# Routing folded into its neighbour blocks: the first layer's beside the time steps, the second layer's in pieces among the projections

## What is computed

```
xn     = (x - mean(x)) / sqrt(var(x) + 1e-5)
logits = xn @ router + bias;  prob = softmax(logits)          # 8 experts
layer 0: e = argmax(prob);            gate = prob[e]
layer 1: e0, e1 = the two largest;    position of each token in its expert's list, dropped at 512
time steps: dt = softplus(logits_dt + dt_bias);  a = -dt * exp(A_log);  sums of a inside chunks of 128
layer 1:  q = xn @ Wq;  latent = (xn @ (Wk + Wv)) @ W_down;  k = latent @ W_up_k;  v = latent @ W_up_v
```

## Time and profile before

| what | value |
| --- | --- |
| median of 3 runs | 2052.54 us |
| profiled execution | 2049.56 us, span 2047.8 us |
| TensorE busy | 1803.0 us, 88% of the span |
| VectorE busy | 1381.2 us, 67% |
| ScalarE busy | 1159.0 us, 57% |
| GpSimd busy | 432.4 us, 21% |
| mean granted TensorE clock | 0.94 of full speed |

### The profile page before, as it was taken

The page is one execution under the profiler, slowest core; times in us unless marked ns, Lnnn a source line. Parts: engine busy times, 40 slices in busy tenths (PEclk is TensorE's granted clock), DMA queues, the critical chain, the costliest instruction groups (busy, mean ns, idle before and its releaser), DMA issues. The chain is left out here.

```text
span 2047.8 us, 33896 instructions
## 1 busy us (share of the span) xinstructions
PE 1803.0 (88%) x10070; PEld 1240.1 (61%) x10070; DVE 1381.2 (67%) x3090; ACT 1159.0 (57%) x2806; POOL 432.4 (21%) x406
## 2 busy tenths in 40 slices
PE   5389999999999889999844988999999898999998
PEld 2247657656766679999812454555556464656555
DVE  5648678768677612222165869798879888888885
ACT  2145665665565412222111538888888888888886
POOL 2004413422432334321110111020201002020101
PEclk9689899899899889999966999999999999999999
DMA  4412212312221188655173583252424333343311
GB/s 165 137 55 93 92 63 79 105 61 72 92 72 62 42 300 276 201 180 173 54 236 117 159 260 106 73 104 73 104 73 93 63 83 94 83 93 83 86 29 32
DMA packets 143790, 226.12 MB, mean 110 GB/s; under 512 B 17725, under 2 KB 110015, under 8 KB 143648
## 3 DMA queue, kind: packets, MB, share of 16 engines
q1 hardware_dynamic: 124464, 179.95, 29.1%
q0 software_dynamic: 19184, 44.45, 8.5%
HBM read 174.26 MB, written 50.99 MB: 110 GB/s over the span
## 5 line engine op out<-in xcount | busy, mean ns | idle before, releaser
L2286 DVE TENSOR_SCALAR att_scores<-att_psS 128x512 f32<-128x512 f32 x512 | 352.9, 690 | 95.3 <-PE att_psS L2116 94.8
L2235 ACT ACTIVATE att_prob<-att_scores,att_shift 128x512 f32<-128x512 f32 x512 | 383.2, 748 | 23.0 <-DVE att_shift L2302 22.9
L2244 ACT COPY att_pT<-att_psT 128x512 f32<-128x512 f32 x512 | 306.4, 599 | 132.5 <-PE att_psT L2124 131.9
L2294 DVE CUSTOM_DVE_ANT_0 att_scores<-att_scores,first_decay 128x512 f32<-128x512 f32 x512 | 352.0, 688 | 0.0
L2124 PEld LDWEIGHTS att_psT<-ident,att_prob 128*128 128x128 f32 x2048 | 244.8, 142 | 158.7 <-issue 97.6
L2124 PE MATMUL att_psT<-ident,att_prob 128*128 128x128 f32 x2048 | 315.1, 277 | 15.4 <-ACT att_pT L2244 14.8
L2116 PE MATMUL att_psS<-first_ks,first_qs 128*128 128x512 bf16 x512 | 195.8, 384 | 17.3 <-DVE att_scores L2286 13.5
L1123 ACT ACTIVATE mamba_L<-mamba_am,mamba_minus 128x128 f32<-128x128 f32 x512 | 153.9, 387 | 44.5 <-PE mamba_psY L998 44.4
L2138 PE MATMUL att_psO<-att_pT,att_v 128*32 128x512 f32 x1024 | 140.6, 624 | 37.8 <-ACT att_pT L2244 37.8
L1543 ACT ACTIVATE ffn_hT<-ffn_psH,ffn_b 128x128 f32<-128x128 f32 x156 | 44.7, 369 | 194.6 <-PE ffn_psH L1499 194.6
L1499 PEld LDWEIGHTS ffn_psH<-ffn_xT,ffn_w 128*128 128x128 f32 x1248 | 145.3, 192 | 3.6 <-DMA ffn_w<-in_w 0.9
(11 more groups left out here) (287 smaller groups left out, 2872.4 us busy)
## 6 DMA issues: line engine op xcount, KB each, us to landing
ffn_w<-in_w SPq DMA_DIRECT2D x39, 1024.0 KB, 5.6
mamba_am<-a_rows SPq DMA_DIRECT2D x64, 512.0 KB, 3.8
first_qs<-q_parts SPq DMA_DIRECT2D x256, 64.0 KB, 3.1
first_ks<-k_parts SPq DMA_DIRECT2D x256, 64.0 KB, 3.1
xn<-xn_all SPq DMA_DIRECT2D x16, 512.0 KB, 5.7
ffn_w<-in_w POOLq DMA_DIRECT2D x8, 1024.0 KB, 6.7
att_w<-in_inter POOLq DMA_DIRECT2D x7, 1024.0 KB, 5.5
att_w<-in_outer POOLq DMA_DIRECT2D x7, 1024.0 KB, 7.3
```

The lines of the kernel that those rows point to most:

```text
L2235: nc.scalar.activation(prob[:, n % NP], scores[:, n % NCL], ACT.Exp, bias=shift[:, h % 2, t:t + 1], accum_out=total[:, octet % 2, t, j, i: ...
L2244: nc.scalar.copy(pT[:, h % HEADS_T, :, t * P:(t + 1) * P], bank_of("turn", n)[:].rearrange("p (k q) -> p k q", k=CPB)).then_inc(pT_ready, 1)
L2286: vec.tensor_scalar(scores[:, n % NCL], psS[n % NS][:], -CLAMP, CLAMP, ALU.max, ALU.min).then_inc(clipped, 1)
L2294: vec.tensor_tensor_reduce(scores[:, n % NCL], scores[:, n % NCL], decay[:, FAR - t * P:FAR - t * P + SEQ], 1.0, -2.0 * CLAMP, ALU.mult, A ...
```

## The change

It takes `route` apart into a class `Router`, whose methods are pieces of the same arithmetic, with a few `step`s turned into `link`s. In layer 0 the pieces stand inside the block of the time steps. In layer 1 they stand inside `project`, each after or between VectorE's takes and subtractions of a named batch. The two rank matmuls stand on TensorE behind the values of batch 2, and the first quarter of the table product behind those of batch 6. The latent's PSUM tile has one bank in place of two, to make room for `psR`. The matrix `hot_row` holds one pick in place of two, so that the second pick's quarters wait for the first pick's products (`used`). In layer 1 the stores of `xn_all` go into the normalisation.

```diff
@@ normalise
                     if merge:
                         sp.wait_ge(merged, (b + 1) * CPB)
                         sp.dma_start(rows(merge[2], b), x[:, b]).then_inc(x_kept, 16)
+                        sp.wait_ge(xn_ready, (b + 1) * CPB)
+                        sp.dma_start(rows(xn_d, b), xn_all[:, b * CPB:(b + 1) * CPB, :]).then_inc(xn_kept, 16)
...
@@ class Places
-        self.hot_row = s.sb(f"{name}_hot_row", [P, picks, NT, P])
+        self.hot_row = s.sb(f"{name}_hot_row", [P, NT, P])
...
+        if k:
+            dve.wait_ge(self.used, quarter + 1)
...
+class Router:
...
+    def exponentials(self, act):
+        act.wait_ge(self.shifted, 1)
+        self.nc.scalar.activation(self.prob[:], self.lb[:], ACT.Exp).then_inc(self.prob_exped, 1)
+
+    def ranks(self, pe):
+        pe.wait_ge(self.chosen, 1)
+        self.nc.tensor.matmul(self.ps_rank, self.C.before, self.mask[:], start=True, stop=True)
+        self.nc.tensor.matmul(self.ps_tile, self.C.ones[:], self.mask[:], start=True, stop=True).then_inc(self.ranked, 1)
...
+    def shift(self, dve):
+        c, v = self.c, self.nc.vector
+        dve.wait_ge(self.bias_in, 16)
+        dve.wait_ge(self.order_counted, 3)
+        c.link(v.tensor_copy(self.order[:], self.order_i[:]))
+        c.link(v.tensor_copy(self.rowbase[:], self.rowbase_i[:]))
+        c.link(v.tensor_copy(self.tiles[:], self.tile_i[:]))
+        c.step(v.tensor_tensor(self.lb[:], self.logits[:, :, 0:NE], self.per_expert(self.bias[:]), ALU.add))
...
@@ route_and_steps (time_steps before)
                 sp.dma_start(neg_a[:], a_log_bc).then_inc(loaded, 16)
+                router.load(sp)
+                for b in range(BATCH):
+                    sp.dma_start(xn_d[b * SEQ:(b + 1) * SEQ, :].rearrange("(c p) d -> p c d", p=P),
+                                 xn_all[:, b * CPB:(b + 1) * CPB, :]).then_inc(rows_stored, 16)
...
+                router.ranks(pe)
                 pe.wait_ge(a_ready, 2)
...
+                router.exponentials(act)
                 act.wait_ge(w_ready, 1)
...
+                router.chained(dve)
+                router.shift(dve)
                 dve.wait_ge(exped, 2)
                 v.tensor_scalar(w[:], u[:], 1.0, None, ALU.add).then_inc(w_ready, 1)
+                router.probabilities(dve)
+                router.pick(dve, 0)
+                router.choose(dve)
...
+                router.rank_all(dve)
+                router.tiles_of(dve)
+                router.first_slots(dve)
                 dve.wait_ge(decay_ready, 1)
...
@@ project
                 sp.dma_start(wuv[:], w["wuv"]).then_inc(w_in, 16)
+                router.load(sp)
                 first.load_wo(sp)
...
-                    if b >= 2:
-                        pe.wait_ge(lat_ready, b - 1)
+                    pe.wait_ge(lat_ready, b)
...
                     values(b)
-                pe.wait_ge(lat_ready, BATCH - 1)
-                for k in range(2):
-                    for q in range(4):
-                        table.multiply(nc, pe, psL[0][:, 0:2 * table.columns], k, q)
+                    if b == 2:
+                        router.ranks(pe)
+                    elif b == BATCH - 2:
+                        table.multiply(nc, pe, psR[:, 0:2 * table.columns], 0, 0)
+                for q in range(1, 4):
+                    table.multiply(nc, pe, psR[:, 0:2 * table.columns], 0, q)
+                for q in range(4):
+                    table.multiply(nc, pe, psR[:, 0:2 * table.columns], 1, q)
...
                 v.tensor_tensor(wkT[:], wkT[:], wvT[:], ALU.add).then_inc(joined, 1)
+                router.chained(dve)
+                router.shift(dve)
...
                     if b:
                         subtract(K, b - 1)
                         take_low(Q, b - 1)
+                    if b == 1:
+                        router.pick(dve, 1)
+                    elif b == 3:
+                        router.rank_all(dve)
+                    elif b == 4:
+                        router.second_slots(dve, 0)
+                    elif b == 5:
+                        table.columns_hot(nc, dve, choice, 1)
+                    elif b > 5:
+                        quarter = 2 * (b - 5) - 1
+                        table.rows_hot(nc, dve, choice, quarter // 4, quarter % 4)
                     if b < BATCH:
                         take(K, b)
                         subtract(Q, b)
                     if b:
                         take_low(K, b - 1)
-                    if b < 2:
-                        table.columns_hot(nc, dve, choice, b)
-                    if b < BATCH:
-                        table.rows_hot(nc, dve, choice, b // 4, b % 4)
-                table.take(nc, dve, psL[0], places)
+                    if b == 0:
+                        router.probabilities(dve)
+                        router.pick(dve, 0)
+                    elif b == 2:
+                        router.choose(dve)
+                    elif b == 3:
+                        router.passes(dve)
+                    elif b == 4:
+                        router.second_slots(dve, 1)
+                        table.columns_hot(nc, dve, choice, 0)
+                    elif b > 4:
+                        quarter = 2 * (b - 5)
+                        table.rows_hot(nc, dve, choice, quarter // 4, quarter % 4)
+                table.rows_hot(nc, dve, choice, 1, 3)
+                table.take(nc, dve, psR, places)
...
@@ build
-                route(nc, C, "route1", logits, a["br1_bc"], xn_all, xn1_d, False, choice1)
-            project(nc, C, xT_all, a, qp_d, kp_d, v_d, first, choice1, places1)
+            project(nc, C, xT_all, a, logits, qp_d, kp_d, v_d, first, choice1, places1)
```

321 lines of the change are left out of this document (162 added, 159 removed).

## The result

The changed kernel takes **2040.96 us** (median of 10 runs, 2030.34 to 2048.72); the kernel before, beside it, 2054.66 us (10 runs, 2051.78 to 2065.50). The ratio is 0.9918, with a 95% interval of 0.9892 to 0.9943 (the quotient of the two medians is 0.9933). The forecast was 2030.7 us with a range of 2018 to 2042, and 0.40 for a change within 1%.

What follows compares the result with a forecast made beforehand. VectorE's chain was taken to bound the routing, TensorE to pace `project`. Terms -13.0 - 25.5 + 0.3 + 16.4 = -21.8 us took 2049.56 to 2027.8; the median, 3 higher, 2030.7; range 2018 to 2042, by term bounds 2025 to 2036.

Steps and rivals of the forecast that it cites:

- Layer 0, gain 13.0: Layer 0's routing and time steps in one block: VectorE's waits get cover, gain 13.0 us, bounds 11 and 14.
- Layer 1, the block, gain 25.5, and the stores at nothing: Layer 1's routing block goes, gain 25.5 us; the `xn_all` stores moved into the normalisation cost nothing.
- The rival in which the stores hold up the loads: Layer 1's normalisation: stores delay loads by 11.6 us, total 2042; chance 0.15 shared with routing not hidden.
- step 3: Project, batch 2: TensorE waits 3.1 us for the mask, rank matmuls take 2.16, batch 3's queries start 5.3 late.
- Step 4: Project from batch 3 on: VectorE has no free time, its work sums to 59.1 us.
- the routing hides: Rival in project: VectorE's free time suffices, only the 5.3 us at the rank matmuls return; 2019.6, chance 0.08.
- Step 5: Project: GpSimd's four column scalings each hold up VectorE, 4.4 us; counted as seen, one in four, 1.5.
- the forecast's 14.57: End of project: 14.57 us from the store that waits for keys 6's low part to the next block.
- the clock falls once: Rival: batch 2's wait halves TensorE's clock, queries cost up to 3.7 more (2034.4), block start up to 2; chance 0.14.
- TensorE is not what the end waits for: End of project: hence moving the first table quarter behind batch 6 was held to be worth nothing.
- Faster by over 1%: Outcome for the whole kernel: a time below 2032.0 us, chance 0.55.
- The slower rival: Project, batches 3 to 7: TensorE's clock stays at 1.2 GHz, VectorE hiding much below a point; 2080, chance 0.05.

Runs made afterwards that it cites:

- after: The changed kernel as it is, first profile; 2040.96 us, ratio 0.9918 to the kernel before.
- l0_only: The kernel before with the layer 0 part of the change alone; 2048.23 us, ratio 0.9957.
- no_reads: The changed kernel with GpSimd's four scalings replaced by memsets that read no memory, so layer 1's places are zeros; 2025.05 us, ratio 0.9903.
- again: The changed kernel, unaltered, for a second profile; 2040.16 us, ratio 0.9901 to the kernel before.
- after_third: The changed kernel, unaltered, for a third profile; 2040.48 us, ratio 0.9925 to the kernel before.
- l1_only: The changed kernel with layer 0's two old blocks, so layer 1's part alone; 2053.22 us, ratio 0.9987 to the kernel before.
- later_warm: ranks_later with 128-column products that nothing uses put on TensorE at the start and end of project; 2017.62 us, ratio 0.9879.
- parts_first: later_warm with the last batch's low parts ahead of its first row matrix on VectorE; 2032.82 us, ratio 0.9898.
- before_third: The kernel before, unchanged, profiled on the same chip as after_third; 2050.01 us in its one execution.
- ranks_later: The changed kernel with the two rank matmuls behind the queries of batch 3 instead of the values of batch 2; 2037.69 us, ratio 0.9901.
- before_again: The kernel before, unchanged, for a second profile; 2048.62 us, ratio 1.0015.

## Why the prediction came out as it did

**Layer 0, gain 13.0: right.** The stage up to Mamba fell by 13.3 (after) and 14.1 (l0_only). From the end of the last logits to Mamba's first load it is 30.2 us (50.68 to 80.91) against 44.7 (49.46 to 94.2), 14.5 less; the logits themselves came 1.2 us later. Over all profiles it is 43.0 to 44.8 us in the four with the two old blocks and 30.2 to 30.4 in the nine with the new one, a gain of 12.6 to 14.6. The forecast was some 32 us.

**Layer 1, the block, gain 25.5, and the stores at nothing: right.** From the last logits to project's first load it is 1.5 us in place of 26.6, a gain of 25.1. (That the load is issued 26.2 us earlier in after is chance: layer 0's gain, a longer expert stage and a shorter normalisation are in it.) Normalisation and block fell from 89.8 to between 61.6 and 65.2; less 25.5 they would be 64.3. The rival in which the stores hold up the loads is out.

**Project, step 3, the wait for the mask: right, but for the clock behind it.** TensorE waits 3.11 us (forecast 3.1), and it is 1.86 from the first rank matmul to the queries (2.16, already at the lower clock).

**Step 4, no free time from batch 3 on: right.** From the take of the queries of batch 3 to the last row matrix I forecast 59.1 + 4.4 = 63.5 us; it took 63.4 or 63.5 in all eight profiles of the table in which GpSimd scales, wherever TensorE's clock fell. In after VectorE's idle time over this stretch is 0.96 us, in pieces of at most 0.1. The rival "the routing hides" is out.

**Step 5, GpSimd, 4.4: right**, 4.1 by no_reads. In the trace of before one scaling in four had held VectorE; in the new order all four did. By the Trainium skill ("SBUF — State Buffer", Who interferes with whom) a VectorE instruction with two inputs in SBUF and a GpSimd instruction that reads SBUF exclude each other, and the trace agrees: all four stretched operations have two such inputs, each ends 1.07 to 1.09 us after the scaling beside it, and without scalings (no_reads) none is stretched. A count of what was seen would have given 1.5.

**The clock: the step that failed.** Project was to take 116.7 us and took 122.7, 121.4, 119.6 and 121.7 in the four profiles of after's code (after, again, after_third, l1_only). The table of points says where. At the start the first queries begin at 11.6, 11.8, 9.8 and 11.9 in place of 9.7: the fall of the clock there comes in three of these four. Behind the mask the take comes 5.7, 4.2, 4.5 and 4.3 us after the queries begin, in place of 3.74. At the end it is 8.9 to 9.0 from the rows to the close in place of 6.6: the table product at half rate closes the block, while the store path would have at some 120 in after (the store of keys 6 at 1198.58, and the forecast's 14.57). For the profile of after that is 3.6 late at the take and 2.4 at the end, 6.0 in all; for after_third 0.6 and 2.3. The first two falls stood in the prediction as a rival, "the clock falls once", with up to 3.7 and 2. I gave it 0.14, although showed a clock of 0.57 after 3.6 us without a matmul and I had just forecast a wait of 3.1. It should have been part of the forecast. The third I excluded with the sentence that TensorE is not what the end waits for. That held at full clock only: 3.18 us of waiting behind the rows at full clock became 7.18. Holding the clock does not give all of it back, though: later_warm and parts_first close 7.6 and 8.0 us behind the rows, not 6.6, since from the store of keys 6 to the next block they take 15.6 and 16.0 us in place of 14.57.

**The level.** The measured time lies in the range of 2018 to 2042 with 1 us to spare, and outside the 2025 to 2036 that the bounds of the terms gave. Faster by over 1%, to which I gave 0.55, did not come; within 1%, with 0.40, did. By stages after gained 18.5 us and after_third 16.3 against before_third. The three ratios say -16.8, -20.4 and -15.4 us. The forecast's 2030.7 is 10.3 us below the measured 2040.96: the kernel before measured 2.1 us higher than my base, and the medians differ by 13.7 in place of 21.8. With 2.9 to 6.0 us for the clock in it the forecast of -21.8 becomes -18.9 to -15.8.

**The profiled execution** looked as if nothing had been gained because Mamba and the expert stage differ between executions more than the change is worth. The pair from one chip, with Mamba at 625.0 and 625.6, differs by 22.6 us in span, 4.4 of them in attention.

**The slower rival**, a clock that stays low, did not come in its size. In after the clock is at half rate for some 33 of project's last 116 us (summed over stretches of 2 us): at the start, behind the mask, in batch 4 (0.61 from 1168 to 1172) and at the end. In batch 4 VectorE hides it, as that rival said.

## What to carry to other kernels

Work moved onto an engine that has free time on average is paid for where it stands. Go through the batches, find the one in which TensorE is made to wait, and price the wait with the clock behind it: here 3.1 us of waiting cost 5.4 us of the block, and moving two matmuls behind the next product took that back. The variant with that and the idle products (later_warm) is the best version by project (112.5 against 122.7) and has the lowest ratio, 0.9879, though its interval overlaps that of after. And where a profile shows one exclusion between VectorE and GpSimd, count the pairs that the new order makes, not those that were seen.

## What the runs showed of the hardware that was not expected

**A clock that stays at half rate under unbroken work.** From 1199.74 TensorE works 13.90 us without a gap on 128x56 table products and its granted clock stays at 0.50, in after and again in no_reads, ranks_later and after_third. In before the same products come with the clock at 1.00 and keep it there for their 14.50 us. In after the products of 512 columns behind the first latent were at full clock again with the queries at 1104.38 (3.70 us). A record of the table product takes 0.217 us at 0.50 and 0.113 to 0.132 at 1.00.

**A fall that comes or not.** At the start of project TensorE waits for the same copy in the six profiles of the changed project that have no idle products there, and the first latent behind it takes some 3.5 us or 1.93. The length of the wait does not tell which. The latent takes 3.38 us behind a wait of 1.67 (after), 3.54 behind 1.58 (again), 3.59 behind 1.73 (ranks_later) and 3.68 behind 0.38 (l1_only, which had waited 2.57 us one product earlier). But it takes 1.93 behind 1.47 (after_third) and 1.93 behind 1.71 (no_reads). What decides is not shown. TensorE's timeline in after_third:

```profile
1090.68 1.93 PE L1749 MATMUL proj_psL<-xT_all,proj_wkv 128*64 128x512 f32 x4 [1.47 <-DVE proj_wkv L1882]
1092.54 3.70 PE L1756 MATMUL proj_psQ<-xT_all,proj_wq 128*128 128x512 f32 x8
```

and in no_reads:

```profile
1083.76 1.93 PE L1751 MATMUL proj_psL<-xT_all,proj_wkv 128*64 128x512 f32 x4 [1.71 <-DVE proj_wkv L1884]
```

**The clock's part in the spread.** Mamba takes 636.1 us with a mean clock of 0.93 in before_again and 625.0 with 0.95 in before_third, the kernel being the same. Busy time by stretch, before_again and before_third:

```profile
94.20:730.30 636.10, 590.02 (x2946) 413.85 (x2947) 444.69 (x624) 349.94 (x873) 207.11 (x189) 0.93 0.23 79
```
```profile
91.60:716.60 625.00, 578.96 (x2947) 406.66 (x2947) 443.17 (x624) 349.96 (x873) 209.93 (x189) 0.95 0.24 80
```

The two come from different chips, but ranks_later and l0_only, from one chip and with the same Mamba code, differ as much (636.1 and 625.5). TensorE's busy time differs by 11.06 us, the whole difference, and VectorE's by 1.5. An effect below 1% is better read from the stages that the change touches than from whole executions.
